# Attention scores from float32 parts in two rounded pieces, two heads in the two 64-row halves of TensorE

## What is computed

```
x = x + 0.5 * ffn(layernorm(x))     # mixture of 8 experts, 2 per token
x = x + attn(layernorm(x))          # below
x = x + 0.5 * ffn(layernorm(x))     # the same experts again

# attn: 16 heads of 16 features
c_q, c_kv = x @ W_dq, x @ W_dkv                    # 64 latents each
Q, K, V = c_q @ W_uq, c_kv @ W_uk, c_kv @ W_uv     # (4, 1024, 16, 16)
scores = where(causal, Q @ K^T / sqrt(16), -inf)
out = softmax(scores) @ V @ W_o
```

## Time and profile before

| | |
|---|---|
| time, median of 3 runs | 1254.05 us (1253.89 to 1259.84) |
| span of the profiled execution | 1263.3 us, 22,520 instructions (its own time is not listed apart from the span) |
| TensorE busy | 1066.7 us, 84% |
| VectorE busy | 829.9 us, 66% |
| ScalarE busy | 666.1 us, 53% |
| DMA | 132.53 MB, mean 105 GB/s |

### The profile page before, as it was taken

One profiled execution on the slowest core, in us unless ns is written; L12 is line 12 of the kernel. 1 busy time (PEld: TensorE's weight loads), 2 busy tenths in 40 slices (PEclk: granted clock), 3 DMA queues, 4 the chain that ended last, 5 costly groups with the idle time before them and its releaser, 6 DMA issues. The chain is left out here.

```text
span 1263.3 us, 22520 instructions
## 1 busy us (share of the span) xinstructions
PE 1066.7 (84%) x6988; PEld 642.3 (51%) x6988; DVE 829.9 (66%) x2536; ACT 666.1 (53%) x1668; POOL 384.3 (30%) x404
## 2 busy tenths in 40 slices
PE   3539999984988899999999999999859369999940
PEld 2328888872442244443444444444347258888840
DVE  6774444436867888888888888888037754444427
ACT  5605554542753376676777666667636315455520
POOL 6506777752002000000000000000048227777730
PEclk8559999995977699999999999999889759999985
DMA  9503333326756444444444444440057113333339
GB/s 301 186 9 93 101 105 105 102 84 216 201 200 142 59 60 61 61 61 60 61 61 60 60 61 61 61 60 11 10 189 239 58 38 94 104 102 104 105 118 331
DMA packets 109248, 132.53 MB, mean 105 GB/s; under 512 B 29968, under 2 KB 83664, under 8 KB 109136
## 3 DMA queue, kind: packets, MB, share of 16 engines
q1 hardware_dynamic: 91280, 89.65, 31.2%
q0 software_dynamic: 13632, 37.24, 9.3%
q10 hardware_dynamic: 4224, 4.19, 1.0%
HBM read 82.42 MB, written 48.23 MB: 103 GB/s over the span
## 5 line engine op out<-in xcount | busy, mean ns | idle before, releaser
L1415 ACT ACTIVATE stacks_rows_or_prob<-stacks_bank 128x512 f32<-128x512 f32 (+3 forms) x768 | 326.0, 494 | 144.1 <-PE stacks_bank L1347 118.9
L1429 DVE CUSTOM_DVE_ANT_0 stacks_bank<-stacks_bank,all_causal 128x128 f32<-128x128 f32 (+3 forms) x512 | 245.4, 504 | 33.7 <-PE stacks_bank L1318 30.2
L1432 DVE TENSOR_REDUCE t_maxp<-stacks_bank 128x1 f32<-128x512 f32 x256 | 175.5, 686 | 25.0 <-PE stacks_bank L1318 24.4
L1318 PE MATMUL stacks_bank<-stacks_kst,stacks_qst 96*128 96x512 bf16 (+2 forms) x528 | 160.3, 348 | 8.5 <-DVE t_maxp L1429 4.2
L1358 PE MATMUL stacks_bank<-stacks_rows_or_prob,stacks_turned_or_values 128*32 128x512 f32 (+3 forms) x1536 | 164.5, 500 | 3.0 <-ACT stacks_rows_or_prob L1415 1.1
L1344 PE MATMUL stacks_bank<-stacks_qst,stacks_kst 99*128 99x512 bf16 (+3 forms) x528 | 154.9, 335 | 2.5 <-ACT stacks_rows_or_prob L1415 1.9
L1296 POOL COPY stacks_turned_or_values<-stacks_values 128x512 f32<-128x512 f32 x16 | 9.8, 613 | 427.7 <-DMA stacks_kst<-qk_parts 286.5
L1318 PEld LDWEIGHTS stacks_bank<-stacks_kst,stacks_qst 96*128 96x128 bf16 x528 | 48.5, 98 | 126.9 <-DVE t_maxp L1429 66.6
L653 PE MATMUL be_psG<-b_w,be_xT 128*128 x426 | 112.8, 401 | 0.0
L653 PE MATMUL ae_psG<-a_w,ae_xT 128*128 x426 | 111.9, 398 | 0.0
L1347 PE MATMUL stacks_bank<-all_causal_t,all_ident_bf 128*128 128x128 bf16 x512 | 109.6, 221 | 0.0
(11 more groups left out here) (296 smaller groups left out, 1917.7 us busy)
## 6 DMA issues: line engine op xcount, KB each, us to landing
stacks_qst<-qk_parts SPq DMA_DIRECT2D x66, 128.0 KB, 4.9
stacks_kst<-qk_parts SPq DMA_DIRECT2D x66, 128.0 KB, 7.6
stacks_rows_or_prob<-y_rows SPq DMA_DIRECT2D x16, 512.0 KB, 6.1
s_yk<-y_rows SPq DMA_DIRECT2D x16, 512.0 KB, 9.4
stacks_parts_or_stacks<-qk_parts SPq DMA_DIRECT2D x60, 128.0 KB, 6.2
qk_parts<-stacks_parts_or_stacks SPq DMA_DIRECT2D x16, 384.0 KB, 2.6
qk_parts<-q_parts SPq DMA_DIRECT2D x16, 384.0 KB, 3.4
o_rows<-t_orow SPq DMA_DIRECT2D x32, 136.0 KB, 8.7
```

The source lines that it names most:

```text
L1318: nc.tensor.matmul(psR[bank][:, 0:w], qst[slot][0:KROWS, h, i * P:(i + 1) * P], kst[slot][0:KROWS, h, k0:k0 + w], start=True, stop=True).t ...
L1415: nc.scalar.activation(prob[j % 2][:, h, a:(c + 1) * 512], psS[n % ST_BANKS][:, a - c * 512:512], ACT.Exp, scale=DK ** -0.5).then_inc(exp_ ...
L1429: ins = nc.vector.tensor_tensor_reduce(psR[bank][:, 0:w], psR[bank][:, 0:w], T.causal[:, 512 - w:512], 1.0, -BIG, ALU.add, ALU.max, maxp[: ...
L1432: ins = nc.vector.tensor_reduce(maxp[:, h, col:col + 1], psR[bank][:, 0:w], AX_X, ALU.max)
```

## The change

- Queries and keys are kept in two parts, both float32r (float32 rounded as TensorE takes it): ScalarE's rounded copy, and what VectorE finds left. `take_high` and `middle` are gone. Three products of parts count instead of six, so a head's score is a product over 48 rows, or 50 with the two rows of the maximum.
- The heads of a pair lie in the two halves of the stacks: rows 0 to 63 and 64 to 127. Their products use the two 64-row halves of the array. Units and products narrower than 256 columns are made 256 wide (`ROUNDED_COLS`).
- The mask of a head pair is added by four products of 64 columns (`mask_pair`), two in each half, after both heads' `score_t`, instead of one of 128 columns per head.
- Ones in `kst` are now written over rows 32 to 63 of each half before the stacks are loaded over rows 32 to 47, so SP waits for them (`ones_ready`).
- The split of the maxima is two instructions instead of five; four rows are copied to `qst` instead of three.
- The parts are stored as float32: 512 KB per transfer instead of 384 KB. The stacks' loads stay at 12 transfers of 128 KB.
- `plan_step` knows the halves: two products in different halves may run at once, a change between halves and the full array costs `SWITCH`, and a mask pair `MASK`.

```diff
-PARTS = 3
-Q_PARTS = (0, 0, 0, 1, 1, 2)
-K_PARTS = (0, 1, 2, 0, 1, 0)
+PARTS = 2
+Q_PARTS = (0, 0, 1)
+K_PARTS = (0, 1, 0)
...
+HALVES = 2
+HALF_ROWS = P // HALVES
+ROUNDED_COLS = 256
...
+ISSUE = 30
+MASK = 120
+SWITCH = 100
...
     def load(self, sp, g, slot):
...
+                by_half = src.rearrange("(c a d) t -> a d c t", a=HALVES, d=DK)
+                for a in range(HALVES):
+                    at = a * HALF_ROWS + r * DK
+                    sp.dma_start(st[slot][at:at + DK, :, :].bitcast(F32), by_half[a]).then_inc(self.loaded[slot], 16)
...
             if c == S // W:
+                sp.wait_ge(Q.ones_ready, HALVES * (SLOTS - 1))
                 stacks(0)
...
             def low(u):
-                dve.wait_ge(mid_ready, c * NU + u + 1)
-                nc.vector.tensor_tensor(parts[b][:, u, 2, :], bank(c, u)[:], parts[b][:, u, 1, :], ALU.subtract).then_inc(low_ready, 1)
+                dve.wait_ge(high_ready, c * NU + u + 1)
+                nc.vector.tensor_tensor(parts[b][:, u, 1, :], bank(c, u)[:], parts[b][:, u, 0, :], ALU.subtract).then_inc(low_ready, 1)
...
     units = []
-    for h in range(HG):
+    for pair in range(HG // HALVES):
         for i in range(QT):
             end = (i + 1) * P
-            units.append((h, i, 0, min(end, 512), i))
-            if end > 512:
-                units.append((h, i, 512, end - 512, i + QT // 2))
+            for k0 in range(0, end, 512):
+                for a in range(HALVES):
+                    units.append((pair * HALVES + a, i, k0, min(end - k0, 512), i + k0 * QT // (2 * 512)))
...
         def load_max(g, slot):
-            wait(sp, m_ready, g + 1)
-            for part in range(PARTS):
-                sp.dma_start(qst[slot][KROWS + part:KROWS + part + 1, :, :], mparts[:, part, :]).then_inc(m_loaded, 16)
+            wait(sp, drained, max_at(g))
+            for a in range(HALVES):
+                at = a * HALF_ROWS + KROWS
+                rows = slice(a * (MROW // HALVES), (a + 1) * (MROW // HALVES))
+                for part in range(PARTS):
+                    sp.dma_start(qst[slot][at + part:at + part + 1, :, :].bitcast(F32),
+                                 mparts[rows, part, :].bitcast(F32)).then_inc(m_loaded, 16)
...
         sp.wait_ge(Q.v_done, 2 * Q.CH)
         load_max(0, 0)
+        sp.wait_ge(Q.ones_ready, HALVES * SLOTS)
         A.load(sp, 2, 2)
...
-        nc.tensor.matmul(psR[bank][:, 0:w], qst[slot][0:KROWS, h, i * P:(i + 1) * P],
-                         kst[slot][0:KROWS, h, k0:k0 + w], start=True, stop=True).then_inc(filled, 1)
+        w = max(w, ROUNDED_COLS)
+        nc.tensor.matmul(psR[bank][:, 0:w], A.rows(qst, slot, h, KROWS)[:, i * P:(i + 1) * P],
+                         A.rows(kst, slot, h, KROWS)[:, k0:k0 + w], start=True, stop=True).then_inc(filled, 1)
...
-            if a == j * P:
-                ins = nc.tensor.matmul(ps[:, 0:P], T.ident_bf[:], T.causal_t[:], start=False, stop=True)
-            ins.then_inc(st_done, 1)
+            ins = nc.tensor.matmul(psS[n % ST_BANKS][:, wide - c * 512:512], A.rows(kst, k, h, MROWS)[:, j * P:(j + 1) * P],
+                                   A.rows(qst, k, h, MROWS)[:, wide:(c + 1) * 512], start=True, stop=a > j * P)
+            if a > j * P:
+                ins.then_inc(st_done, 1)
+
+        def mask_pair(j, c, pair):
+
+            for part in range(HALVES):
+                for a in range(HALVES):
+                    n = n_st[j, c, pair * HALVES + a]
+                    at = j * P - c * 512 + part * HALF_ROWS
+                    rows = slice(a * HALF_ROWS, (a + 1) * HALF_ROWS)
+                    ins = nc.tensor.matmul(psS[n % ST_BANKS][:, at:at + HALF_ROWS], T.causal_halves[rows, part + 1 - a, :],
+                                           T.ident_bf[rows, rows], start=False, stop=part == HALVES - 1)
+                    if part == HALVES - 1:
+                        ins.then_inc(st_done, 1)
...
-            nc.vector.tensor_scalar(neg[:], psR[bank][0:MROW, 0:P], -1.0, None, ALU.mult).then_inc(drained, 1)
-            dve.wait_ge(drained, r + 1)
-            link(nc.vector.tensor_copy(mparts[:, 0], neg[:]), g, 2)
-            link(nc.vector.tensor_tensor(mid[:], neg[:], mparts[:, 0], ALU.subtract), g, 3)
-            link(nc.vector.tensor_copy(mparts[:, 1], mid[:]), g, 4)
-            nc.vector.tensor_tensor(mparts[:, 2], mid[:], mparts[:, 1], ALU.subtract).then_inc(m_ready, 1)
+            turned = psR[bank][0:MROW, 0:P]
+            link(nc.vector.tensor_scalar(mparts[:, 0], turned, -1.0, None, ALU.mult), g, 2)
+            nc.vector.scalar_tensor_tensor(mparts[:, 1], turned, -1.0, mparts[:, 0], ALU.mult,
+                                           ALU.subtract).then_inc(drained, 1)
```

175 lines of the change are left out of this document (102 added, 73 removed).

## The result

The changed kernel takes 1462.9 us (median of 5 runs, 1452.44 to 1528.94) against 1254.05 for the kernel before, a ratio of 1.160 with a 95% interval of 1.155 to 1.166.

What follows compares the result with a forecast made beforehand. TensorE was taken as the bound, 28.7 of 31.1 us a group, VectorE next. Gains of 41 us in steady groups, 2 in the last and 4 in projections gave 1207 us, range 1185 to 1238 (all low or high ends: 1174, 1246).

Steps and rivals of the forecast that it cites:

- TensorE's load: Attention, per group of four heads: summed product costs fall from 28.7 to 25.1 us, ends 21.7 and 26.7.
- The low value for score pairs: Attention score products: 8.1 us a group if halves work side by side; 11.2 if weight loads set the pace; 10.5 taken.
- What is lost beyond the larger load? ... I take 2.7.: Attention, per group: waiting added to VectorE's 25.7 us, the larger load; 2.4 us read from the kernel before, 2.7 taken.
- The forecast period of 28.4: Attention: time per group, 28.4 us, a gain of 2.7 on each of 15 steps, 41 us; bounds 26.5 and 30.5.
- Masks: Attention, per group: 64 mask products of 64 columns cost 2.9 us, between 1.9 in pairs and 3.8 in turn; before 1.9.
- rival 4: Attention: clock falls to 1.2 GHz for a third of the stage, period 35.9, 72 us slower, about 1322; chance 0.04.
- Rival 2: Attention: the two halves' products follow each other instead of running side by side, period 34.1, 1297 us; chance 0.11.
- Rivals 1 and 3: Attention: VectorE the only wall, 1176 us, chance 0.17; new waits replace the old, 1247 us, chance 0.08.
- The maxima's path: Between groups: split 0.7 us shorter, one more transfer issue of 0.59; about 0.5 us a group may show, inside the 2.7.
- Last group: Attention's last group: TensorE load falls by some 4 of 20 us, ScalarE chain remains; gain 2 us, ends 0 and 4.
- Projections: Projection steps: fewer products and copies gain 7 us, larger stores cost 3; net gain 4 us, ends -1 and +7.

Runs made afterwards that it cites:

- masks at once: Changed kernel with each masked tile's two mask products right behind its score product, in its own half, order planned anew: 1299.0 us, ratio 1.032.
- the new interleaving: Changed kernel with each tile's masks right behind its score product and a written-out order of products in the 14 steady groups: 1249.5 us, ratio 0.992.
- the old data in the same late-mask order: Kernel before, with its three bf16 parts and full-array products, but attention products in the changed kernel's order: 1311.2 us, ratio 1.041.
- the kernel with pair units: Kernel before with only VectorE's score tiles reordered, two heads' tiles side by side: 1259.7 us, ratio 1.004.
- a zero product: Changed kernel plus ten full-array products of zeros a group, ahead of output sets: 1361.8 us, ratio 1.082.
- the second execution: Changed kernel, nothing altered, profiled again because its first profiled execution was slow: 1464.7 us.

## Why the prediction was wrong, step by step

- **TensorE's load.** The sum gave 28.7 before and 25.1 after; replayed without waits they are 30.6 and 26.6. Each was short by 1.5 to 1.9, the difference right: 3.6 forecast, 4.0 measured. The low value for score pairs was nearer: 48 pairs at 0.231 and 0.123 against my 0.234 at any width, an estimated 8.9 us instead of 10.5. Output sets with their changes of shape took more, 26.5 - 14.8 = 11.7 against 10.4, and about 3 us of the load stand in no single price.
- **"What is lost beyond the larger load? ... I take 2.7."** This step failed, in its size, and with it the term that stood at nothing in the forecast, the clock (below). I read 2.4 us of waiting out of before's group and carried it over; it was 0.7. At the full clock TensorE waits 8.7 us beyond its load in the changed order, 34.6 - 26.5 - 2.2 = 5.9 with masks at once, and 29.9 - 26.5 = 3.4 in the new interleaving (if that order needs 26.5 too, which was not replayed), not far from my 2.7. How I read it: before, TensorE was the only bound and ran full; with its load cut to 26.6 beside VectorE's, which is (45.06 / 50) x 29.9 = 26.9 in the new interleaving (25.7 in my sum), no engine has a lead, and every late bank shows. That the order decides is shown, by 34.0 against 29.9; this reason for it is not. The forecast period of 28.4 belongs to an order that this change did not have.
- **Masks.** I costed them as products, 2.9 us, where the replay gives 26.5 - 24.4 = 2.1, and did not charge that the tiles of a pair wait for the third and the last of four. I wrote that ScalarE "waits at times". Its idle time ahead of the exponentials went from 144.1 to 351.4 us, and the edit that takes 149.5 of these away is worth 164 us.
- **The clock**, rival 4, chance 0.04, is what happened. "For a third of the stage" was mis-sized: with a mean of 0.65 between the levels 0.50 and 1.00 it stood at the low one for about 0.7 of the time from 420 to 1100 us, and the period is 44.2, not 35.9. My row against it, 905 to 922 us with TensorE busy 13.25 of 17 at 1.00, held for full-array products that run while masks and scores come singly; it was no measure for another order. Its second cause as I put it, more pauses, is borne out in so far as the orders in halves hold 1.00 without waits, full-array products lose the clock with them, and the clock rose when the order waited less (8.7, 5.9 and 3.4 us a group). Its first, half-used rows, stays open: the old data in the same late-mask order kept 1.00, but it also waits only 3.8 us a group, and one half alone ran at 0.50 without a wait.
- **Rival 2** (halves in turn) is refuted by 0.231 us a pair. **Rivals 1 and 3** did not come.
- **The maxima's path.** Inside the excess, as said; no run isolated it.
- **Last group**, gain 2 forecast: it lost 20.8 us in the changed kernel (55.9 us for 35.1), and in the new interleaving, whose last group keeps its planner's order, it still took 897.0 - 846.5 = 50.5 us, with the clock at 0.50 to 0.57 from 856 us on. There, too, the clock is a term that was missing; no run holds it up there alone.
- **Projections**, gain 4: the first join came at 397.7 to 404.3 us in eleven profiles with the changed projections, and at 402.0 to 416.0 in four with the old ones, on average 400 against 411: a gain of some 11 us where I took 4. The steady steps went as written. The wait for the parts' store, "no shorter" in my list, was shorter, 2.36 for 4.28, and the 3 us that I charged for larger stores show in no row. The spread of the old ones is the clock's: the kernel with pair units joined at 402.0 with 306 to 324 us at 1.00, before at 416.0 with 0.55.

The 199 us between the spans, then, as an estimate in which a zero product costs its 0.22 us and does nothing but hold the clock: at the full clock the changed order would have a period of 37.5 - 2.2 = 35.3. The clock is then 15 x (44.2 - 35.3) = 134 us, at least 100 even if the zero products cost nothing (1463 to 1362). Another 15 x (35.3 - 31.2) = 62 are 8.0 us more waiting a group less 4.0 of load. The last group adds 21, and the earlier first join takes 15 off.

What stays open: what makes the clock fall in this order, and whether half-used rows have a share in it; why the clock does not return in the cold stretches, where the second execution has TensorE busy 48.77 of 50 us (ends of products are modelled, so short waits may hide in it), while pairs without waits come back to 1.00 behind a pause; why full-array masks raise the clock and hardly the speed; and how late masks and the new cost model share the 51.5 us.

## What to carry to other kernels

Before cutting the load of the engine that bounds, replay its instruction order without waits and compare with the period: what is then between them is the real waiting. It can grow with the cut (0.7 to 8.7 us here), so the order must be made anew with it, and for the old data as well: that alone gave 1238.8 us. A pair that is released together holds its banks together; release each tile as soon as it is done. A TensorE that waits more often can lose its clock and with it far more than the waits.

## What the runs showed of the hardware that was not expected

- Two 64-row halves with 48 rows each hold the clock at 1.00 as pairs; one half alone, without a wait, runs at 0.50 (70 products of 512 columns in 30.23 us from a pause, where 70 pairs take 18.03).
- Half products issued a, a, b, b are as fast as a, b, a, b: 160 products from 365.47 to 383.92 us, 0.115 each.
- Half or full array, the clock fell alike when each product waited: 0.82 and 0.81. With waits of half products one at a time it was 0.83 at 62.12 us busy of 71.7, with pairs 1.00 at 38.89 of 50.
- Ten full-array products of zeros a group, estimated at 2.2 us, held the clock at 1.00 from 500 us on in an order that has a mean of 0.65 without them.
- The kernel with the same half products took, by their order and by when the masks come, from 1249 to 1463 us.
